# Attention over two layers on one core: single-head exponentials in three banks, four banks for the maxima jobs, and TensorE's order written out

## The chip, the cores and the metric

One core of a Trainium2 chip runs the whole kernel. The metric is the time of one execution on the device in microseconds (us), the median of several runs. TensorE (PE in the profile) multiplies matrices into PSUM, which has eight banks of 512 fp32 columns; VectorE (DVE) and ScalarE (ACT) read PSUM; GpSimd (POOL) works on SBUF; SP issues the transfers.

## The reference

The input x has 4 sequences of 1024 rows of 128 values. Four blocks follow, each added to x: attention a, a feed-forward block, attention b (causal), the same feed-forward block. Each works on the rows after a layer norm. Both attentions have 16 heads of 8 values.

```python
x = x + attn_a(layernorm(x))     # softmax(q k^T / sqrt(8)) v, then Wout
x = x + ffn(layernorm(x))        # (silu(x Wg^T) * (x Wu^T)) Wd^T, hidden 384
x = x + attn_b(layernorm(x))     # the same with keys after the query masked out
x = x + ffn(layernorm(x))
```

## The kernel before

An attention is worked off in 16 windows: a window is one sequence and four heads. Its two halves f are the query chunks of 512. For the softmax the kernel first finds each query's largest score, then computes the scores again, transposed, with that maximum taken off inside the product.

- A **job** (`run_job`, L995 on TensorE) is the scores of 128 queries of one head against up to 512 keys, into one PSUM bank. VectorE reduces it to a maximum per query (L785; where the causal mask cuts the block, L782). A window has 64 jobs in the first layer (`PLANS[0]`) and 48 in the second (`PLANS[1]`, widths 128 to 512). Jobs run in a ring of three banks, 4 to 6: the load of job k waits (`ring_free`) until VectorE has finished job k-3. In the first layer they go head by head, two key halves each.
- When the jobs of a half are through, VectorE negates the maxima (L791), GpSimd splits them (L463, L465), TensorE transposes them (the **shift**, L1027), ScalarE copies them (L575) and SP writes them as two more rows of the query operand `qop` (L373). The scores of that half wait for this transfer (`shift_loaded`).
- A **step** is one half against one block of 128 keys: 16 steps in the first layer, 12 in the second, where the triangular ones are narrower and get mask matmuls (L1017). In it the **scores** (L1009) are made for two heads at a time, a **unit**, into two banks; two units take turns, banks 0, 1 and 2, 3. ScalarE makes the exponentials of both heads in one instruction (L559).
- The weighted **sums** (L1045) multiply the step's exponentials by the values, in four column strips at once, into bank 7. They come one step behind. The values are copied for each window into `vwin` by GpSimd (L454).
- At the end of a half ScalarE copies the sums out (L566), TensorE transposes them (the **norm**, L938), ScalarE copies the result (L580), VectorE takes the reciprocal (L796) and multiplies (L801).

Heads with an even number use the lower 64 rows of the array, those with an odd number the upper 64; I call these the row halves 0 and 1. Jobs and scores use a row half each; sums, shifts and norms use all rows.

`Plan` decides what stands between what. It spreads the jobs over a step's four places in the proportions of `SLOT_WEIGHTS`, by width, so that in the first layer each step reads: job, two scores, two jobs, two scores, job, sums. In `turn` every engine walks through the plan in the same order. TensorE issues in that order, and each instruction waits for its own semaphores, so what stands behind a waiting one waits as well.

Of the kernel before, what the change touches and what calls it, by code (L numbers as in the profile page):

```python
# [13 lines left out]
P = 128  # L14
# [15 lines left out]
HG = 4  # L30
# [15 lines left out]
RING = 3  # L46
PROBS = 6
SLOT_WEIGHTS = (1, 1, 1, 0)
# [3 lines left out]
class Plan:  # L52
# [9 lines left out]


    def __init__(self, causal, turn, cut, idle_steps, lead, project_at):
        self.causal = causal
        self.turn = turn
# [12 lines left out]
        for f in range(2):  # L79
            for qb in range(TPC):  # L80
                for c in range(HG):
                    width = (TPC * f + qb + 1) * P if causal else S
                    for kh in range(2):
                        w = min(width - kh * CHUNK, CHUNK)
                        if w > 0:
                            stream.append((f, c, qb, kh, w, causal and kh * CHUNK + w == width))
        cut = len(stream) if cut is None else cut
        jobs = [(0, x) for x in stream[cut:]] + [(1, x) for x in stream[:cut]]
        self.turn_steps = [(0, s) for s in range(turn, n)] + [(1, s) for s in range(turn)]

        slots = [0 if i >= n - idle_steps else weight * (CHUNK - self.steps[s][2])
                 for i, (_, s) in enumerate(self.turn_steps) for weight in SLOT_WEIGHTS]
        total_c, total_s = sum(x[4] for _, x in jobs), sum(slots)
        placed, k, done_c, done_s = [], 0, 0, 0
        for w in slots:
            done_s += w
            slot = []
            while k < len(jobs) and (done_c + jobs[k][1][4] / 2) * total_s <= done_s * total_c:
                slot.append(jobs[k])
                done_c += jobs[k][1][4]  # L100
                k += 1
            placed.append(slot)
        assert k == len(jobs)
        self.turn_jobs = [placed[4 * i: 4 * i + 4] for i in range(n)]

        self.turn_ends = [[] for _ in range(n)]
        for i, (dw, s) in enumerate(self.turn_steps):

            if (dw, s) == (0, self.half_end[0] + 2):
                self.turn_ends[i].append((0, "norm", 0))  # L110
            if (dw, s) == (1, 1):
                self.turn_ends[i].append((0, "norm", 1))
            for jw, x in (y for slot in self.turn_jobs[i] for y in slot):
                if self.ends_half(x):
                    self.turn_ends[i + 1].append((jw, "shift", x[0]))


        units = [("exp", s, pair) for s in range(turn) for pair in range(2)]
        events, due, start = [], {}, None
        for k, x in enumerate(stream[:cut]):  # L120
            events.append(("job", x))
            if self.ends_half(x):
                due[k + 4] = ("shift", x[0])
                start = k + 4 + lead if x[0] == 0 else start
            if k in due:
                events.append(due.pop(k))
            elif start is not None and k >= start and (k - start) % 3 == 0 and units:
                events.append(units.pop(0))
        self.before = events + units + list(due.values())


        self.project_at = project_at
        own = [i for i, (dw, _) in enumerate(self.turn_steps) if dw == 0]
        self.last_jobs = [[[x for x in slot if x[0] == 0] for slot in self.turn_jobs[i]] for i in own]
        self.last_ends = [[x for x in self.turn_ends[i] if x[0] == 0] for i in own]
        self.units_before = sum(kind != "job" for kind, *_ in self.before)
        self.units_turn = 2 * n + sum(map(len, self.turn_ends))
        self.units_all = (self.units_before + (WINDOWS - 1) * self.units_turn + 2 * len(own)
                          + sum(map(len, self.last_ends)) + 1)
        self.jobs_before, self.jobs_turn = cut, len(jobs)  # L140
        self.jobs_all = WINDOWS * len(stream)
        assert self.units_turn % 2 == 0

    def ends_half(self, job):
        f, c, qb, kh, _, _ = job
        return (c, qb, kh) == (HG - 1, TPC - 1, 0 if self.causal and f == 0 else 1)


PLANS = [Plan(causal=False, turn=3, cut=32 + 22, idle_steps=0, lead=7, project_at=(6, 8, 11)), Plan(causal=True, turn=2, cut=None, idle_steps=1, lead=12, project_at=(2, 4, 8))]


def transformer_pair_kernel(nc, x_in, wqkv_a, bqkv_a, wout_a, bout_a, wqkv_b, bqkv_b, wout_b, bout_b,
# [10 lines left out]
    with ExitStack() as ctx:  # L163
# [121 lines left out]
        def windows(eng, body, turns):  # L285

            for w in range(turns):
                body(w, w % BUFS, w // BUFS)
# [913 lines left out]
```

## Time and profile before

| | |
|---|---|
| median of 3 runs | 1573.65 us (1570.76 to 1574.26) |
| profiled execution | 1573.21 us, of which the span from first to last instruction is 1571.4 us |
| first layer's attention | about 73 to 820 us |
| second layer's attention | about 944 to 1478 us |
| TensorE, VectorE, ScalarE busy | 92%, 79%, 62% of the span |
| mean granted TensorE clock | 0.965 of 2.4 GHz |

A timeline row gives start, duration, engine, line, operation, destination and source, and how many instructions it merges; in brackets the idle time before it and who ended it. PEld is the load of a matmul's stationary operand, which carries the wait. Ends of matmuls are modelled.

### The profile page before, as it was taken

The numbers are of one execution on the slowest core, as the hardware profiler recorded it, in microseconds if no ns is written. First come the engines' busy times: TensorE is split into PE (matmuls) and PEld (weight loads), VectorE is DVE, ScalarE is ACT, GpSimd is POOL, SyncE is SP. The second block draws the span as 40 slices with busy tenths as digits, with TensorE's granted clock in tenths as the row PEclk, the third lists the DMA queues.
The fourth block names the chain that finished last, engine by engine and source line by source line (L and its number), as shares of the span: only waits on it lengthen the run. The fifth ranks groups of instructions, "written<-read, shape, count | busy, mean of one in ns | idle before, by whom it ended". The sixth has DMA issues, their size and how long they took to land.

```text
span 1571.4 us, 26128 instructions
## 1 busy us (share of the span) xinstructions
PE 1438.6 (92%) x9625; PEld 701.7 (45%) x9625; DVE 1235.9 (79%) x3106; ACT 980.0 (62%) x1259; POOL 108.9 (7%) x210
## 2 busy tenths in 40 slices
PE   3699999999999999999988988999999999999888
PEld 2444344434444443444436654444444444444455
DVE  7589999999999998999937757787787877777254
ACT  4427777777777777777774432666666666666622
POOL 6020000000000000000001112000000000000010
PEclk9859999999999999999999985999999999999999
DMA  3720111111101111110001323111121112210000
GB/s 95 221 57 7 27 28 29 29 29 28 28 6 25 28 28 29 28 28 2 2 1 54 83 79 76 35 29 29 29 53 32 29 29 47 38 29 2 8 21 27
DMA packets 40055, 58.39 MB, mean 37 GB/s; under 512 B 7796, under 2 KB 19448, under 8 KB 39928
## 3 DMA queue, kind: packets, MB, share of 16 engines
q1 hardware_dynamic: 39928, 56.72, 15.2%
q8 instruction: 76, 1.25, 0.3%
q14 instruction: 51, 0.42, 0.1%
HBM read 36.77 MB, written 18.87 MB: 35 GB/s over the span
## 4 chain that ended last, share of the span: by engine, by line
PE 70%; DVE 18%; ACT 5%; issue 4%; DMA 2%; SPq 1%; POOL 0%; DVEq 0%; ACTq 0%; POOLq 0%
PE psum L995 25%; PE psum L1045 23%; DVE maxima L785 11%; PE psum L1009 6%; PE psum L1142 5%; PE psum L938 4%; ACT probs L559 3%; DVE junk L782 3%; PE psum L1147 2%; PE psum L1017 1%; PE psum L948 1%; DVE xn L706 1%; PE psum L1062 1%; DMA k_parts<-parts 1%; DMA qop<-shift_rows 1%
## 5 line engine op out<-in xcount | busy, mean ns | idle before, releaser
L559 ACT ACTIVATE probs<-psum 128x1024 f32<-128x1024 f32 (+3 forms) x896 | 794.2, 932 | 300.4 <-PE psum L1009 192.7
L785 DVE TENSOR_REDUCE maxima<-psum 128x1 f32<-128x512 f32 x1280 | 815.2, 684 | 72.8 <-PE psum L995 67.8
L995 PE MATMUL psum<-kop,qop 62*128 62x512 f32 (+3 forms) x1792 | 657.0, 465 | 56.5 <-DVE maxima L782 20.0
L1009 PE MATMUL psum<-qop,kop 64*128 64x512 f32 (+3 forms) x1792 | 498.2, 411 | 10.4 <-ACT probs L559 7.8
L995 PEld LDWEIGHTS psum<-kop,qop 62*128 62x128 f32 x1792 | 289.6, 191 | 487.6 <-DVE maxima L785 325.4
L1045 PE MATMUL psum<-probs,vwin 128*32 128x512 f32 (+3 forms) x3584 | 441.6, 565 | 3.9 <-ACT probs L559 2.0
L782 DVE CUSTOM_DVE_ANT_0 junk<-psum,mask 128x384 bf16<-128x384 f32 (+3 forms) x512 | 237.4, 487 | 75.3 <-PE psum L995 69.8
L1009 PEld LDWEIGHTS psum<-qop,kop 64*128 64x128 f32 x1792 | 242.0, 189 | 55.7 <-ACT probs L559 44.7
L1045 PEld LDWEIGHTS psum<-probs,vwin 128*32 128x32 f32 x3584 | 71.8, 109 | 105.5 <-issue 84.6
L1017 PE MATMUL psum<-half_ident,key_mask 64*128 64x64 bf16 x1024 | 92.7, 198 | 0.0
L1142 PE MATMUL psum<-ffn_xt,wffn 128*128 128x512 f32 x192 | 87.6, 594 | 0.0
L463 POOL TENSOR_TENSOR shift<-negmax,zeros 128x16 bf16<-128x16 f32 x64 | 14.1, 220 | 1017.5 <-DVE negmax L791 1017.5
L796 DVE RECIPROCAL rden<-att_raw 128x16 f32<-128x16 f32 x64 | 15.8, 247 | 61.3 <-ACT att_raw L580 61.3
L656 ACT ACTIVATE hid<-psum 128x512 f32<-128x512 f32 x48 | 28.7, 597 | 52.0 <-PE psum L1142 52.0
L1147 PE MATMUL psum<-wffn,hid 128*128 128x128 f32 x384 | 48.7, 278 | 7.9 <-DVE hid L899 7.9
L1017 PEld LDWEIGHTS psum<-half_ident,key_mask 64*128 64x128 bf16 x1024 | 49.7, 97 | 13.1 <-issue 1.3
L899 DVE TENSOR_TENSOR hid<-psum,hid 128x512 f32<-128x512 f32 x48 | 32.4, 689 | 26.8 <-PE psum L1142 21.4
L1147 PEld LDWEIGHTS psum<-wffn,hid 128*128 128x128 f32 x384 | 45.2, 192 | 15.4 <-DVE hid L899 15.4
L575 ACT CAST shift_rows<-psum 32x128 f32<-32x128 bf16 x64 | 16.3, 254 | 56.7 <-PE psum L1027 56.7
L714 DVE TENSOR_TENSOR x<-psum,x 128x512 f32<-128x512 f32 x32 | 22.1, 690 | 37.4 <-PE psum L1147 29.1
L1142 PEld LDWEIGHTS psum<-ffn_xt,wffn 128*128 128x128 f32 x192 | 34.2, 191 | 31.9 <-issue 31.0
L938 PEld LDWEIGHTS psum<-ident,sums 128*128 128x128 f32 x256 | 26.8, 140 | 44.9 <-ACT probs L559 40.2
(88 smaller groups left out, 709.9 us busy)
## 6 DMA issues: line engine op xcount, KB each, us to landing
qop<-q_parts SPq DMA_DIRECT2D x256, 64.0 KB
q_parts<-parts SPq DMA_DIRECT2D x32, 256.0 KB, 3.0
k_parts<-parts SPq DMA_DIRECT2D x32, 256.0 KB, 3.4
kop<-k_parts SPq DMA_DIRECT2D x64, 128.0 KB
kop<-k_parts SPq DMA_DIRECT2D x128, 64.0 KB
x<-in_L_attn_a_x SPq DMA_DIRECT2D x8, 256.0 KB, 4.4
qop<-shift_rows SPq DMA_DIRECT2D x128, 8.0 KB
out_x<-x SPq DMA_DIRECT2D x8, 256.0 KB, 2.3
```

Of the source, the lines that this page charges most:

```text
L559: nc.scalar.activation(probs[:, slot, :, c0:], psum[:, bank:bank + 2, c0:], ACT.Exp, scale=SCORE_SCALE).then_inc(probs_ready, 1)
L656: nc.scalar.activation(hid[:, c, :], psum[:, 2 + 2 * (c % 2), :], ACT.Silu).then_inc(silu_ready, 1)
L782: nc.vector.tensor_tensor_reduce(out=junk[:, slot, 0:width], in0=src, in1=mask[:, CHUNK - width:], scale=1.0, scalar=LOWEST, op0=ALU.add, ...
L785: nc.vector.tensor_reduce(dst, src, AX_X, ALU.max).then_inc(ring_free, 1)
L899: nc.vector.tensor_tensor(hid[:, c, :], psum[:, 3 + 2 * (c % 2), :], hid[:, c, :], ALU.mult).then_inc(hid_ready, 1)
L938: ins = nc.tensor.transpose(psum[:, bank, t * P:(t + 1) * P], src[:, t, :], ident[:])
L995: mm(psum[:, slot, 0:width], qop[rows, buf, f, r, qb * P:(qb + 1) * P].bitcast(F32R), kop[rows, buf, r, kh * CHUNK:kh * CHUNK + width].bit ...
L1009: ins = mm(psum[:, bank + h, c0:], kop[rows, buf, pair, j * P:(j + 1) * P].bitcast(F32R), qop[rows, buf, f, pair, c0:].bitcast(F32R), star ...
L1017: ins = mm(psum[:, bank + h, at:at + TILE_ROWS], key_mask[rows, part, :], half_ident[rows], start=False, stop=part == 1)
L1045: ins = mm(psum[32 * c:32 * c + 32, 7, c0:], vwin[:, buf, at:at + 32], probs[:, slot, c % 2, c0:], start=(j == 0), stop=(s == plan.half_en ...
L1142: mm(psum[:, 2 + 2 * (c % 2) + k, :], wffn[:, k, c, :], ffn_xt[:], start=True, stop=True).then_inc(gate_up_psum, 1)
L1147: ins = mm(psum[:, 7, t * P:(t + 1) * P], hid[:, c, t * P:(t + 1) * P], wffn[:, 2, c, :], start=(c == 0), stop=(c == FB - 1))
```

## The change

The plan is now a string of letters for each layer, walked by every engine: j is a job, s the scores of one unit, p the sums of the step that stands `sums_behind` steps back, H and h the shifts of this window's second and the next window's first half, N and n the norms.

In the first layer a unit is one head in one bank, `unit_ring=3`: banks 0 to 2; `job_ring=4`: banks 3 to 6. A step has four units and four exponentials of 512 columns. In the second layer units stay pairs in two double banks and jobs in three, but jobs are listed with `alternate=True`, so that neighbours use different row halves. The jobs run 48 ahead in the first layer and 44 in the second. The sums read `v` itself; `vwin` and its copies are gone. SP's loads of window w + 2 now come behind window w's second shift.

```diff
-RING = 3
-SLOT_WEIGHTS = (1, 1, 1, 0)
+PROB_STEPS = PROBS // 2
...
+                tiles = [(c, kh) for r in range(PAIRS) for kh in range(2) for c in (2 * r, 2 * r + 1)] if alternate \
+                    else [(c, kh) for c in range(HG) for kh in range(2)]
...
+    def bank(self, unit):
+        return unit % self.unit_ring * len(self.heads[0])
...
-PLANS = [Plan(causal=False, turn=3, cut=32 + 22, idle_steps=0, lead=7, project_at=(6, 8, 11)), Plan(causal=True, turn=2, cut=None, idle_steps=1, lead=12, project_at=(2, 4, 8))]
+PAIR_UNITS, HEAD_UNITS = ((0, 1), (2, 3)), ((0,), (1,), (2,), (3,))
+PLANS = [Plan(causal=False, heads=HEAD_UNITS, unit_ring=3, job_ring=4, alternate=False,
+              order="jsjjsspjssjsjpjsjsjnsjjsspjssjsjpjsjsjsjjsspjssjsjpHjsjsjsjjsspjssjsjpjsjsjsjjsspjssjsjpjsjsjNsjjsspjssjsjpjsjsjsjjsspjssjsjphjsjsjsjjsspjssjsjpjsjs",
+              jobs_ahead=48, sums_behind=2, project_at=(9, 11, 14)),
+         Plan(causal=True, heads=PAIR_UNITS, unit_ring=2, job_ring=3, alternate=True,
+              order="sjjsjpjsjsjpjjjHsjjsjpjsjjspjjsjsjsjjnjjspjsjsjjpjsjjsjpjjsjsjpjjsjNjjsphjjspjjjspjjspjs",
+              jobs_ahead=44, sums_behind=1, project_at=(4, 6, 10))]
...
                 for kind, w, number, f in plan.walk:
                     if kind == "shift":
-                        shift_to_operand(what[0], 0, unit)
...
+                        shift_to_operand(f, w % BUFS, unit_base + number)
+                        if f == 1 and w + 2 < WINDOWS:
+
+                            wait(sp, sums_done, sums_base + w * plan.n)
+                            load_operands(w + 2, (w + 2) % BUFS)
...
-                def exp_unit(w, wmod, s, pair, unit, static_unit):
+                def exp_unit(w, number, s, heads):
...
+                    if heads[0] == 0 and step >= PROB_STEPS:
+
+                        act.wait_ge(sums_done, sums_base + step + 1 - PROB_STEPS)
+                    nc.scalar.activation(probs[:, slot, heads[0] % 2:heads[-1] % 2 + 1, c0:], psum[:, bank:bank + len(heads), c0:],
+                                         ACT.Exp, scale=SCORE_SCALE).then_inc(probs_ready, 1)
...
-                        ins = mm(psum[32 * c:32 * c + 32, 7, c0:], vwin[:, buf, at:at + 32], probs[:, slot, c % 2, c0:],
+                        ins = mm(psum[32 * c:32 * c + 32, 7, c0:], v[:, at:at + 32], probs[:, slot, c % 2, c0:],
```

On TensorE, in the middle of the first layer, one step of before stands between two sums like this (L995 jobs, L1009 scores, L1045 sums):

```order
L1045 MATMUL psum<-probs,vwin 32x512 x4
L995 MATMUL psum<-kop,qop 128x512
L1009 MATMUL psum<-qop,kop 128x512 x2
L995 MATMUL psum<-kop,qop 128x512 x2
L1009 MATMUL psum<-qop,kop 128x512 x2
L995 MATMUL psum<-kop,qop 128x512
L1045 MATMUL psum<-probs,vwin 32x512 x4
```

There are four jobs and four scores between any two sums. In the changed kernel the same engine has, at the same place (L876 jobs, L890 scores, L924 sums), a group of ten, of which this is the whole:

```order
L924 MATMUL psum<-probs,v 32x512 x4
L876 MATMUL psum<-kop,qop 128x512
L890 MATMUL psum<-qop,kop 128x512
L876 MATMUL psum<-kop,qop 128x512
L890 MATMUL psum<-qop,kop 128x512
L876 MATMUL psum<-kop,qop 128x512
L890 MATMUL psum<-qop,kop 128x512
L876 MATMUL psum<-kop,qop 128x512 x2
L890 MATMUL psum<-qop,kop 128x512 x2
L924 MATMUL psum<-probs,v 32x512 x4
```

Behind its sums stands a group of six: job, two scores, job, score, job. The two kinds take turns, and a norm or shift goes into or ahead of one of ten.

In the second layer, on TensorE, before has in the middle of a window's second half (L938 is the norm):

```order
L1045 MATMUL psum<-probs,vwin 32x512 x4
L938 MATMUL psum<-ident,sums 128x128 x4
L995 MATMUL psum<-kop,qop 128x128
L995 MATMUL psum<-kop,qop 128x512
L1009 MATMUL psum<-qop,kop 128x512 x2
L995 MATMUL psum<-kop,qop 128x128
L995 MATMUL psum<-kop,qop 128x512
L1009 MATMUL psum<-qop,kop 128x512 x2
L995 MATMUL psum<-kop,qop 128x256
L995 MATMUL psum<-kop,qop 128x512
L1045 MATMUL psum<-probs,vwin 32x512 x4
```

It holds six jobs, and the group ahead of it and that behind it hold six as well. The changed kernel has there:

```order
L924 MATMUL psum<-probs,v 32x384 x4
L876 MATMUL psum<-kop,qop 128x128
L890 MATMUL psum<-qop,kop 128x512 x2
L876 MATMUL psum<-kop,qop 128x512
L890 MATMUL psum<-qop,kop 128x512 x2
L876 MATMUL psum<-kop,qop 128x512
L876 MATMUL psum<-kop,qop 128x128
L924 MATMUL psum<-probs,v 32x512 x4
L876 MATMUL psum<-kop,qop 128x128
L890 MATMUL psum<-qop,kop 128x512 x2
L876 MATMUL psum<-kop,qop 128x512 x2
```

The sums follow after four jobs instead of six. Ahead of this piece stands one long group of eight jobs, four pairs of scores and a norm.

## Rows read from the trace of the kernel before

**Rows 1.** The page, part 1: busy us, share of the span, instructions
```profile
PE 1438.6 (92%) x9625; PEld 701.7 (45%) x9625; DVE 1235.9 (79%) x3106; ACT 980.0 (62%) x1259; POOL 108.9 (7%) x210
```

**Rows 2.** The page, part 4: the chain that ended last, by line
```profile
PE psum L995 25%; PE psum L1045 23%; DVE maxima L785 11%; PE psum L1009 6%; PE psum L1142 5%; PE psum L938 4%; ACT probs L559 3%; DVE junk L782 3%; PE psum L1147 2%; PE psum L1017 1%; PE psum L948 1%; DVE xn L706 1%; PE psum L1062 1%; DMA k_parts<-parts 1%; DMA qop<-shift_rows 1%
```

**Rows 3.** Line L566, two stretches: duration min/median/max, first and last start
```profile
L566 ACT COPY sums<-psum x31: 585/587/596, 130.9 to 800.5; 128x512 f32<-128x512 f32 x31
L566 ACT COPY sums<-psum x21: 585/594/596, 1113.7 to 1431.3; 128x512 f32<-128x512 f32 x21
```

**Rows 4.** Waits from 200 to 700 us: total us, times, longest
```profile
PEld psum L995 <- DVE maxima L785: 213.5, 334, 0.8
```

**Rows 5.** Waits from 1010 to 1390 us
```profile
PEld psum L995 <- DVE maxima L782: 75.1, 155, 1.2
```

**Rows 6.** Timeline of one first-layer step, weight loads left out
```profile
410.17 0.51 PE L995 MATMUL psum<-kop,qop 62*128 62x512 f32 x1
410.17 0.74 PE L1009 MATMUL psum<-qop,kop 64*128 64x512 f32 x2
410.54 0.60 PE L995 MATMUL psum<-kop,qop 62*128 62x512 f32 x2
410.71 1.89 DVE L785 TENSOR_REDUCE maxima<-psum 128x1 f32<-128x512 f32 x3 [0.22 <-PE psum L995]
410.88 0.50 PE L1009 MATMUL psum<-qop,kop 64*128 64x512 f32 x2
410.94 1.94 ACT L559 ACTIVATE probs<-psum 128x1024 f32<-128x1024 f32 x2 [0.77 <-PE psum L1009]
411.46 0.50 PE L995 MATMUL psum<-kop,qop 62*128 62x512 f32 x1
411.88 1.07 PE L1045 MATMUL psum<-probs,vwin 128*32 128x512 f32 x8
412.88 0.50 PE L995 MATMUL psum<-kop,qop 62*128 62x512 f32 x1
```

**Rows 7.** Timeline: a norm between two steps
```profile
423.72 0.66 PE L938 MATMUL psum<-ident,sums 128*128 128x128 f32 x4
...
424.30 0.50 PE L995 MATMUL psum<-kop,qop 62*128 62x512 f32 x1
```

**Rows 8.** Exponentials of 512 elements: two in a row, and all (busy, mean ns)
```profile
1456.15 1.09 ACT L559 ACTIVATE probs<-psum 128x512 f32<-128x512 f32 x2
...
L559 ACT ACTIVATE probs<-psum 128x512 f32<-128x512 f32 x64 | 36.7, 597 | 31.0 <-PE psum L1017 30.9
```

**Rows 9.** Timeline: sums of steps without jobs, last window
```profile
791.93 1.06 PE L1045 MATMUL psum<-probs,vwin 128*32 128x512 f32 x8
...
793.98 1.06 PE L1045 MATMUL psum<-probs,vwin 128*32 128x512 f32 x8
```

**Rows 10.** A stretch: length, busy PE, PEld, DVE, ACT, POOL, granted clock, DMA share, GB/s
```profile
105.00:110.00 5.00, 5.00 (x19) 2.10 (x17) 4.47 (x8) 3.07 (x3) 2.39 (x1) 0.50 0.01 3
```

**Rows 11.** Groups by shape: masked maxima (busy us, mean ns, idle before)
```profile
L782 DVE CUSTOM_DVE_ANT_0 junk<-psum,mask 128x512 bf16<-128x512 f32 x128 | 85.6, 688 | 25.2 <-PE psum L995 22.5
L782 DVE CUSTOM_DVE_ANT_0 junk<-psum,mask 128x128 bf16<-128x128 f32 x128 | 34.2, 286 | 21.6 <-PE psum L995 19.4 <-issue 0.3
```

**Rows 12.** Timeline: sums of four successive steps of the second layer
```profile
1206.00 0.64 PE L1045 MATMUL psum<-probs,vwin 128*32 128x256 f32 x8
...
1208.25 0.85 PE L1045 MATMUL psum<-probs,vwin 128*32 128x384 f32 x8
...
1211.78 1.07 PE L1045 MATMUL psum<-probs,vwin 128*32 128x512 f32 x8
...
1215.47 1.07 PE L1045 MATMUL psum<-probs,vwin 128*32 128x512 f32 x8
```

**Rows 13.** Timeline: a shift, and the first scores that wait for it
```profile
415.47 0.22 PE L1027 MATMUL psum<-ident_bf,shift 128*32 128x128 bf16 x1
...
418.62 0.50 PE L1009 MATMUL psum<-qop,kop 64*128 64x512 f32 x2
```

More of the change, by code:

```diff
@@ L89, in __init__ @@
[L89 to L102, printed above, removed]
@@ L118, in __init__ @@
[L118 to L128, printed above, removed]
@@ L138, in __init__ @@
[L138 to L142, printed above, removed]
[L144 to L149 removed]
+                width = (TPC * f + qb + 1) * P if causal else S
@@ new lines, in __init__ @@
+        assert order.count("j") == len(stream) and order.count("s") == len(units) and order.count("p") == n
+        ends = {"H": ("shift", 0, 1), "h": ("shift", 1, 0), "N": ("norm", 0, 0), "n": ("norm", -1, 1)}
+        self.walk = []
+        jobs = taken = 0
+        last_unit = {}
+        for turn in range(-1, WINDOWS + 1):
+            j, u, k = jobs_ahead, 0, -sums_behind
+            for letter in order:
+                if letter == "j":
+                    w, x = turn + j // len(stream), stream[j % len(stream)]
+                    j += 1
+                    if 0 <= w < WINDOWS:
+                        self.walk.append(("job", w, jobs, x))
+                        jobs += 1
+                elif letter == "s":
+                    w, x = turn, units[u]
+                    u += 1
+                    if 0 <= w < WINDOWS:
+                        self.walk.append(("scores", w, taken, x))
+                        last_unit[w, x[0]] = taken
+                        taken += 1
+                elif letter == "p":
+                    w, x = turn + k // n, k % n
+                    k += 1
+                    if 0 <= w < WINDOWS:
+                        self.walk.append(("sums", w, last_unit[w, x], x))
+                else:
+                    kind, dw, f = ends[letter]
+                    if 0 <= turn + dw < WINDOWS:
+                        self.walk.append((kind, turn + dw, taken, f))
+                        taken += 1
@@ L881, in _ @@
-                invert_denominators(last, 1, unit)
-                scale_sums(last, 1)
+                unscaled, unnegated = [], []
+                for kind, w, number, what in plan.walk:
+                    if kind == "job":
+                        run_job(what, number)
+                    if kind in ("job", "sums", "shift"):
+                        for f, jobs in unnegated:
+                            negate_max(f, job_base + jobs)
+                        for window, f in unscaled:
+                            scale_sums(window, f)
+                        unscaled, unnegated = [], []
+                    if kind == "job" and plan.ends_half(what):
+                        unnegated.append((what[0], number + 1))
+                    if kind == "norm":
+                        invert_denominators(w, what, unit_base + number)
+                        unscaled.append((w, what))
+                    if kind == "scores" and w == WINDOWS - 1 and what[1] == plan.heads[-1]:
+                        early_chunk(what[0])
```

326 lines of the change are left out of this document (82 added, 244 removed).

## The prediction

> **What bounds the kernel now.** I read the page first. TensorE is busy 92% of the span and VectorE 79% [rows 1], but the chain that ended last is TensorE's jobs, TensorE's weighted sums, and VectorE's maxima in turn [rows 2]: a loop through two engines, not one full engine. The starts of the sums copies date the windows: 31 copies from 130.9 to 800.5 are 15 windows of 44.64 us in the first layer, 21 from 1113.7 to 1431.3 are 10 of 31.76 us in the second [rows 3]. In 500 us of the first layer TensorE's weight loads for jobs waited 213.5 us for VectorE [rows 4], in 380 us of the second 75.1 us for the masked maxima alone [rows 5].
>
> One step stands in [rows 6]. TensorE starts a job and the first scores at 410.17; the first job's maximum starts at 410.71, and the ring has three banks, so the step's fourth job waits for that maximum and loads at 411.46. It takes 0.42 to clear the array; the sums start at 411.88 and the next step 1.00 later, at 412.88. The loop is 0.54 + 0.75 + 0.42 + 1.00 = 2.71. VectorE's four maxima come 0.60 apart (three in 1.89, the last 0.69 long), 2.40 a step: it idles 0.22 before them. So 16 x 2.71 = 43.3, and two norms, each adding 0.58 (423.72 to 424.30, [rows 7]), make 44.5 of the 44.64.
>
> The same rows price TensorE. Matmuls of one row half end 0.24 apart: the first ends at 410.68, the scores at 410.91, the next job at 411.14, the last scores at 411.38, while matmuls of the other half run too. So halves run side by side, starts are in program order, and a 512-column matmul costs its half 0.24. A group between two sums costs 0.51 to its first end, 0.24 for each further one on the longer half, -0.07 to the sums (411.46 + 0.50 to 411.88), and 1.00.
>
> **The change, first layer.** The sums now have 3 and 5 jobs (and as many single scores) between them in turn. I write j and s with their row half. Long group: j1 s0 j1 s1 j0 s0 j0 j1 s1 s0; in-order starts put it in 6 places. Short group: j1 s1 s0 j0 s1 j0, 4 places.
> Long: without waits its last end is 0.51 + 5 x 0.24 = 1.71. Two rings bind. The fifth job needs the first's bank: as now, load at 0.54 + 0.75 = 1.29. The fifth scores need the second's bank out of three: first exponential at 0.54; the next 0.49 later (two in 1.09, one 0.60 long, [rows 8]), 1.03; it holds its bank 0.60, and a load follows its releaser by 0.05 to 0.06 (410.71 + 0.69 to 411.46); load at 1.69; sums 0.43 later, 2.12; group over at 3.12.
> Short: 0.51 + 3 x 0.24 - 0.07 = 1.16, plus 1.00 = 2.16; its banks have long been free.
> Two steps take 5.28, VectorE's eight maxima 4.80. A step is 2.64 against 2.71. The fourth bank removes the wait before every sums, but the score ring gives half of it back. A norm now stands inside a long group, after its third job: it starts at 0.51 + 2 x 0.24 - 0.07 = 0.92 and TensorE goes on 0.58 later, at 1.50; what is left, s0 j0 j1 s1 s0, takes 3 places, so the last end is 1.50 + 0.51 + 2 x 0.24 = 2.49 and the sums come at 2.42 instead of 2.12: 0.3 a norm, because the norm fills what was a wait. The rings don't bind there: the second bank's 1.69 is long past. Window: 8 x 5.28 + 2 x 0.3 = 42.85, or 1.8 less; 15 windows give 27 us. ScalarE: 64 exponentials x 0.49 = 31.4 and 3 for copies, under 42.9: hidden. The copies of v on GpSimd that go away were off the chain.
> Against the norm's new place speaks that it empties the array once more: 0.42 - 0.24 = 0.18 before it (a job alone clears the array in 0.42, in a stream costs 0.24) and 0.51 - 0.24 = 0.27 behind it [rows 6]. Without the wait that they fall into, a norm would cost 0.58 + 0.45 = 1.03, and the window would gain 1.8 - 1.4 = 0.4. This is what a rule of the Trainium skill says (TensorEngine Tiling (Array Packing), Key Properties): changing the tiling mode drains TensorE. I keep 0.3.
> Ends. In the last window most steps have no jobs. Now such steps take 2.05 (791.93 to 793.98, [rows 9]); after, long group 0.54 + 0.49 + 0.65 + 0.43 + 1.00 = 3.1 and short 0.51 + 0.24 - 0.07 + 1.00 = 1.7, 2.4 a step: 12 x 0.35 = +4. The prefix runs jobs alone at VectorE's 0.60 and gives 6 jobs less but 3 steps less too; the clock there is at 1.2 GHz (0.50 from 105 to 110, [rows 10]), and the first full steps fall in it: +2, an estimate. First layer: -27 + 6, rounded -20 us.
>
> **The change, second layer.** Three banks and pairs stay; what changes is the order, and jobs now alternate halves. The loop above, with VectorE's times for masked jobs (688 ns for 512 columns, 286 for 128, so 0.134 per 128 columns, each 0.08 less start to start [rows 11]: 0.61, 0.48, 0.34, 0.21), says a group of n jobs takes 0.54 + the first n-3 maxima + 0.15 + 0.42 + the sums (1.00, 0.79, 0.57, 0.36 by width: four passes of 53 ns less for every 128 columns). They are checked by [rows 12], from one sums to the next (the sums in the formula are those that the interval begins with). To 1208.25, four jobs: 0.48 + 1.11 + 0.57 = 2.16, measured 2.25. To 1211.78, six: 0.61 + 0.60 + 0.21 + 1.11 + 0.79 = 3.32, measured 3.53. To 1215.47, six and a norm: 0.21 + 0.60 + 0.21 + 1.11 + 1.00 + 0.58 = 3.71, measured 3.69. So this layer is one ring wait per group, and the more jobs stand between two sums, the longer it is: VectorE idles through the sums, then TensorE waits through its maxima.
> The maxima of a window sum to 16 x 0.60 + 8 x (0.61 + 0.48 + 0.34 + 0.21) = 22.7, with its small operations about 24.2. The new order puts eight jobs, four score pairs and a norm into one long group and two to five jobs into each other one. I walked it with the same rules, carrying VectorE's backlog over each sums.
> The long group: its first job ends at 0.47, and the maxima run on from 0.50 at 0.48, then 0.61 and 0.60 each. Exponentials of a pair start 0.92 apart (two in 1.94, the last 1.02, [rows 6]) and hold their bank 1.02 + 0.05: they start at 0.79 and 1.71, so the third pair loads at 1.86 and the norm at 2.78. It is over at 3.36; the two jobs and the last scores behind it end at 4.10, the sums (384 wide) come at 4.03 and end at 4.8. VectorE has never been idle and has work until 5.2.
> Then, in order: 2.15, 2.05, 2.6, 3.3 (with the other norm), 1.8, 1.65, 1.2, 2.3, 2.3, 1.95, 1.75. With 4.8 that is 27.9. E.g. the group after the long one, j1.128 s s j0.512 s s j1.512 j0.128: the backlog is 0.4, every bank is free before it is needed, last end 0.36 + 0.16 + 3 x 0.24, 1.15 to the sums, + 1.00 = 2.15 where the old order has 3.5 to 3.7. My rules ran short of [rows 12] by 0.09, 0.21 and -0.02, 0.1 on average; on 12 groups that makes 29.1. Gain 2.6 a window, 15 windows: 39. Ends: two more steps in the last window, +3.5; prefix 44 jobs instead of 48 with two steps at half clock, -4.5. Second layer: -40 us.
> Moved too: a half's shift goes through TensorE, ScalarE and SP's queue before its first scores; now that takes 3.15 us from its transpose to the scores that wait for it (415.47 to 418.62, [rows 13]). In the new order 4.0 lie between in the second layer and over 5 in the first, so it hides; were it late, the excess would be paid twice a window. SP's 14 loads of a window now stand behind its second shift instead of ahead of it, a whole window before they are used: nothing.
>
> **Sum.** The profiled execution took 1573.2 (span 1571.4), the median is 1573.65: no difference. 1573 - 20 - 40 = 1513; I say 1515.
>
> **The rivals.**
> 1. The score ring is kinder or the waits merge: VectorE becomes the bound, 2.40 a step and 27 a window in the second layer. First layer 8 x 4.80 + 1.4 = 39.8 (-4.8 a window, 72 less, 6 lost at the ends), second 27 a window (-70): 1437 with both, 1480 for half of the way. For it: four banks cover a sums of 1.00. Against: the load at 1.69 that the score ring forces. Chance 0.1.
> 2. The first layer gains nothing: exponentials 0.60 apart instead of 0.49 lengthen each long group by 0.11 (14 us), and a third of the drain is paid after all (6 us). With the second layer whole it is 1535, with half of its gain 1553. For it: a single exponential's records are 0.60 long, and no first-layer row shows two behind each other. Chance 0.17.
> 3. Slower: single scores lose their side-by-side partner. Today scores come as a pair, one on each half; if a job beside a score does not overlap, or a same-half load is exposed, places become more. Price: a further place is 0.24 in two steps, and there are 128 such pairs of steps: 31 us. From two further places on it decides (1515 + 62 = 1577); with three the time is 1607, and fully serial, 16 places for 10, 1515 + 184 = 1700. Against it, [rows 6] have a job and a score loading at 410.17 together, and the same-half ends 0.24 apart. Chance 0.08.
> It is also what a rule of the Trainium skill would do here (TensorE: Matmul & The Clock Gate, Part 3, The mechanism): a weight load overlaps matmuls in flight only where the row group differs. The trace disagrees with it: its same-half ends stand 0.24 apart, 512 columns at 2.4 GHz being 0.213, with a load between each two.
> 4. The time does not move, the waits only change places: 0.03.
>
> **How the numbers follow.** Likeliest (0.62): both layers gain, 1495 to 1540. A measurement here tells 0.2% (3 us). The range takes in half of rival 1 and most of rival 2: 1485 to 1555. Faster: 0.62 + 0.1 + 0.16 = 0.88; same 0.03; slower 0.09.
>
> **What would show it.** First layer: sums copies 42.9 apart per window; sums alternately 3.1 and 2.15 apart; TensorE's longest wait in the long group for the exponential, not for the maximum. Second: windows near 29, VectorE's share of them up. Wrong: more than 0.24 between same-half ends, exponentials 0.6 apart, or jobs waiting again ahead of each sums.

## The result, and the profile of the changed kernel

The changed kernel takes 1464.33 us (median of 4 runs, 1462.78 to 1466.14); before, run beside it, takes 1573.95 (4 runs, 1570.76 to 1577.89). The ratio is 0.9303, 95% interval 0.9279 to 0.9327: 110 us less, where I had said 1515 and a range from 1485. The forecast had the sign and half of the size.

The page of the changed kernel, part 1, and the chain that ended last, by engine and by line:

```profile
PE 1374.2 (94%) x9625; PEld 683.6 (47%) x9625; DVE 1226.2 (84%) x3106; ACT 1001.4 (68%) x1771; POOL 94.4 (6%) x178
...
PE 82%; DVE 8%; ACT 5%; issue 2%; DMA 1%; SPq 1%; POOL 1%; DVEq 0%; ACTq 0%; POOLq 0%
PE psum L924 26%; PE psum L876 24%; PE psum L890 15%; PE psum L989 5%; DVE maxima L703 4%; PE psum L819 4%; ACT probs L498 4%; PE psum L994 3%; PE psum L829 2%; PE psum L898 2%; DVE xn L624 1%; PE psum L941 1%; DVE junk L700 1%; DMA k_parts<-parts 1%; ACT ot L528 1%
```

VectorE's maxima, 11% of the chain of before [rows 2], are 4% of this one; TensorE's scores went from 6% to 15%. The chain has moved into TensorE. The busy times of VectorE and ScalarE hardly changed [rows 1]: the same work in less idle time.

The sums copies (L505, L566 before) date the windows again. Changed kernel, two stretches, duration min/median/max, first and last start:

```profile
L505 ACT COPY sums<-psum x31: 600/604/607, 129.2 to 746.6; 128x512 f32<-128x512 f32 x31
```
```profile
L505 ACT COPY sums<-psum x21: 580/592/592, 1062.6 to 1341.1; 128x512 f32<-128x512 f32 x21
```

A first-layer window is (746.6 - 129.2) / 15 = 41.16 us against 44.64, a second-layer one (1341.1 - 1062.6) / 10 = 27.85 against 31.76 [rows 3]. Fifteen windows of each give 52 and 59 us; the ends of the layers give about 2 back. Waits of the changed kernel, total us, times, longest; the first three rows from 200 to 700 us, the last three from 960 to 1340:

```profile
PEld psum L876 <- DVE maxima L703: 181.4, 267, 0.8
...
PEld psum L890 <- ACT probs L498: 8.2, 49, 0.2
DVE maxima L703 <- PE psum L876: 4.3, 24, 0.2
```
```profile
PEld psum L876 <- DVE maxima L703: 50.9, 63, 0.8
PEld psum L876 <- DVE maxima L700: 49.4, 122, 0.8
DVE junk L700 <- PE psum L876: 35.6, 94, 0.7
```

The 181.4 us beside the 213.5 of [rows 4] look like little gained, but most of either is no wait for VectorE. The weight loads of the long group that is timed below:

```profile
401.95 0.18 PEld L876 LDWEIGHTS psum<-kop,qop 62*128 62x128 f32 x1 [0.84 <-DVE maxima L703]
...
403.23 0.18 PEld L876 LDWEIGHTS psum<-kop,qop 62*128 62x128 f32 x1 [0.48 <-DVE maxima L703]
```

The first is the load of a group's first job. Such a load comes 1.00 behind the start of the sums in every group that begins with a job, in both kernels, whether the maximum that frees its bank ended 0.07 before it, as here, or 0.43, as for the load at 400.05. Its pause is that of the sums. Of the 181.4 us 152.3 are of this kind; the other 29.1 are 73 fifth jobs, in the long groups without a norm, that load 0.04 after their maximum. Of the 213.5 before, 122.8 are of the first kind and 90.7 are the fourth job of each step. The wait for VectorE inside the groups fell from 90.7 to 29.1 us, and only long groups have it.

VectorE's listed waits are 4.3 us in 500: it runs nearly through, busy 40.5 of a window's 41.2 us, where it was 40.7 of 44.7. One short and one long group, timeline of the changed kernel, weight loads left out, columns as in [rows 6]:

```profile
400.05 0.50 PE L876 MATMUL psum<-kop,qop 62*128 62x512 f32 x1
400.06 0.73 PE L890 MATMUL psum<-qop,kop 64*128 64x512 f32 x2
400.39 0.40 PE L876 MATMUL psum<-kop,qop 62*128 62x512 f32 x1
400.59 3.79 DVE L703 TENSOR_REDUCE maxima<-psum 128x1 f32<-128x512 f32 x6 [0.18 <-PE psum L876]
400.63 0.39 PE L890 MATMUL psum<-qop,kop 64*128 64x512 f32 x1
400.64 0.39 PE L876 MATMUL psum<-kop,qop 62*128 62x512 f32 x1
400.83 4.26 ACT L498 ACTIVATE probs<-psum 128x512 f32<-128x512 f32 x8 [0.60 <-PE psum L890]
400.96 1.07 PE L924 MATMUL psum<-probs,v 128*32 128x512 f32 x8
401.96 0.49 PE L876 MATMUL psum<-kop,qop 62*128 62x512 f32 x1
...
403.57 0.59 PE L890 MATMUL psum<-qop,kop 64*128 64x512 f32 x2
404.09 1.07 PE L924 MATMUL psum<-probs,v 128*32 128x512 f32 x8
...
405.08 0.50 PE L876 MATMUL psum<-kop,qop 62*128 62x512 f32 x1
```

The short group starts at 400.05; its six matmuls end at 400.55, twice 400.79, 401.02, 401.03 (start plus duration; two of the six are merged), three on each half, 0.24 apart. Its sums start 0.91 after it, the next group 1.91 after it. The long group goes from 401.96 to 405.08: 3.12, as worked out. ScalarE's eight exponentials take 4.26 us: starts 0.49 apart and 0.60 for the last would be 4.03, the rest is the wait for the long group's first scores. VectorE's maxima, 0.60 apart, fill 4.8 of the 5.04 of these two steps. A long group that holds a norm takes 3.56 from sums to sums, the others 3.14.

### The profile page after: what moved, and what is told of

It reads as the page before. It is cut to its first block, busy times and chain, and to the rows that moved or that the text cites. A ratio compares the mean times of both kernels' runs of the same rounds, so it can differ in the third digit from the quotient of the medians.

```text
span 1462.5 us, 26609 instructions
## 1 busy us (share of the span) xinstructions
PE 1374.2 (94%) x9625; PEld 683.6 (47%) x9625; DVE 1226.2 (84%) x3106; ACT 1001.4 (68%) x1771; POOL 94.4 (6%) x178
## 4 chain that ended last, share of the span: by engine, by line
PE 82%; DVE 8%; ACT 5%; issue 2%; DMA 1%; SPq 1%; POOL 1%; DVEq 0%; ACTq 0%; POOLq 0%
PE psum L924 26%; PE psum L876 24%; PE psum L890 15%; PE psum L989 5%; DVE maxima L703 4%; PE psum L819 4%; ACT probs L498 4%; PE psum L994 3%; PE psum L829 2%; PE psum L898 2%; DVE xn L624 1%; PE psum L941 1%; DVE junk L700 1%; DMA k_parts<-parts 1%; ACT ot L528 1%
## 5 line engine op out<-in xcount | busy, mean ns | idle before, releaser
L498 ACT ACTIVATE probs<-psum 128x512 f32<-128x512 f32 (+3 forms) x1408 | 833.6, 658 | 216.4 <-PE psum L890 116.3
L703 DVE TENSOR_REDUCE maxima<-psum 128x1 f32<-128x512 f32 x1280 | 805.1, 682 | 20.5 <-PE psum L876 15.0
L876 PE MATMUL psum<-kop,qop 62*128 62x512 f32 (+3 forms) x1792 | 592.4, 449 | 18.0 <-DVE v L643 11.1
L890 PE MATMUL psum<-qop,kop 64*128 64x512 f32 (+3 forms) x1792 | 527.1, 422 | 6.4 <-ACT probs L498 2.5
L876 PEld LDWEIGHTS psum<-kop,qop 62*128 62x128 f32 x1792 | 283.7, 192 | 402.7 <-DVE maxima L703 299.0
L924 PE MATMUL psum<-probs,v 128*32 128x512 f32 (+3 forms) x3584 | 440.4, 564 | 0.6 <-ACT probs L498 0.5
L890 PEld LDWEIGHTS psum<-qop,kop 64*128 64x128 f32 x1792 | 268.7, 187 | 76.1 <-ACT probs L498 45.3
L700 DVE CUSTOM_DVE_ANT_0 junk<-psum,mask 128x384 bf16<-128x384 f32 (+3 forms) x512 | 233.5, 485 | 50.3 <-PE psum L876 46.5
L924 PEld LDWEIGHTS psum<-probs,v 128*32 128x32 f32 x3584 | 70.9, 108 | 101.0 <-issue 67.5
L632 DVE TENSOR_TENSOR x<-psum,x 128x512 f32<-128x512 f32 x32 | 22.1, 690 | 36.8 <-PE psum L994 29.1
L819 PE MATMUL psum<-ident,sums 128*128 128x128 f32 x256 | 41.1, 283 | 5.0 <-ACT sums L505 1.6
```

The source lines that it names most:

```text
L498: nc.scalar.activation(probs[:, slot, heads[0] % 2:heads[-1] % 2 + 1, c0:], psum[:, bank:bank + len(heads), c0:], ACT.Exp, scale=SCORE_SCA ...
L700: nc.vector.tensor_tensor_reduce(out=junk[:, slot, 0:width], in0=src, in1=mask[:, CHUNK - width:], scale=1.0, scalar=LOWEST, op0=ALU.add, ...
L703: nc.vector.tensor_reduce(dst, src, AX_X, ALU.max).then_inc(ring_free, 1)
L819: ins = nc.tensor.transpose(psum[:, bank, t * P:(t + 1) * P], src[:, t, :], ident[:])
L876: mm(psum[:, bank, 0:width], qop[rows, buf, f, r, qb * P:(qb + 1) * P].bitcast(F32R), kop[rows, buf, r, kh * CHUNK:kh * CHUNK + width].bit ...
L890: ins = mm(psum[:, bank + k, c0:], kop[rows, buf, c // 2, j * P:(j + 1) * P].bitcast(F32R), qop[rows, buf, f, c // 2, c0:].bitcast(F32R), ...
```

## The experiments

Times with three rounds have an interval; single ones (E3 to E7) are compared with before's 1570 to 1581. "Two steps" is always one long and one short group, and window lengths are distances of sums copies.

**E1 and E2: one layer at a time.** The other layer gets the order of before, rebuilt as a string of letters, with the reciprocal as late as it was. Here for E1:

```diff
-         Plan(causal=True, ..., alternate=True, order="sjjsjpjsjsjpjjjHsjjsjp...", jobs_ahead=44, ...)]
+         Plan(causal=True, ..., alternate=False, order="sjjsjpsspHnjjjsjjsjpjj...", jobs_ahead=45, ..., late=(6, 0))]
```

> The first layer as in the changed kernel, the second layer with the order of before (jobs not alternating, the reciprocal as late as it was). Theory A (each layer's gain stands by itself, 3.5 us a window in the first): windows of 41.2 us in the first layer and 31.7 in the second, in all 1573 - 54 = 1520 us. Rival (the layers help each other, or the second layer gains from what is common, the missing copies of v and the later loads): second-layer windows clearly under 31.7, below 1505 us.

> The second layer as in the changed kernel; the first layer with the order of before, pairs in two double banks and three job banks. Theory A: windows of 44.6 us in the first layer and 27.9 in the second, in all 1573 - 55 = 1518 us; together with the other half run this makes the whole 109 us. Rival: less than 40 us gained, the rest being common to both.

E1: 1510.3 (1509.65 to 1510.67), ratio 0.9594 (0.9577 to 0.9611). E2: 1517.5 (1516.81 to 1518.62), 0.9640 (0.9619 to 0.9661). So 64 and 56 us, together 10 more than both at once. In E1's trace the first-layer windows are 41.18 as in the changed kernel, but the second layer with its old order has windows of 31.40 instead of 31.74 (5 us in 15), and 162.0 instead of 165.1 us lie between the last sums copy of one layer and the first of the next, where the changed kernel has 166.2. So some 8 us of E1's gain are not the first layer's order, and E1 lands between the theory's 1520 and the rival's 1505. The 5 us stand in windows in which TensorE has the same order as before; the edits outside the order (no `vwin` copies, other times for SP's loads) are left for them, but none was tried by itself. The 3 us needn't be theirs: the rebuilt layer starts another way, with 45 jobs ahead of its first scores where before had 32. In E2 the rebuilt first layer has windows of 44.82 instead of 44.66, 2.5 us in 15. Why the new second-layer order doesn't have the 8 us on top was not separated either.

**E6 and E7: the second layer's order without alternating halves, and the reverse.**

E6 is E1 with the first change here, E7 the changed kernel with the second:

```diff
-              alternate=False, order="sjjsjpsspHnjjjsjjsjp...",
+              alternate=True, order="sjjsjpsspHnjjjsjjsjp...",
...
-              alternate=True, order="sjjsjpjsjsjpjjjHsjjsjp...",
+              alternate=False, order="sjjsjpjsjsjpjjjHsjjsjp...",
```

> The first layer as in the changed kernel; the second with the order of before, but jobs alternate between the row halves. Theory A (the order makes the gain, since jobs waited for banks and not for a half): second-layer windows 31.3 to 31.7 us, 1510 to 1520 in all. Rival (the alternation makes a good part of it): windows under 30 us, under 1495.

> The changed kernel, but in the second layer jobs go head by head. Theory A (the order makes the gain): second-layer windows 27.9 to 28.5 us, 1464 to 1474 in all. Rival (the alternation makes a good part): 29.5 us or more, 1490 or more.

E6: 1531.1, 21 us more than E1, windows 32.2 to 34.9; both its theory (1510 to 1520) and its rival missed. E7: 1471.8, 7 us more than the changed kernel, windows 28.65. The second layer's gain is the order; alternation is worth 7 us with it, and costs 21 with the old one.

E6's 21 us are two things. At full clock its windows are 32.2 against 31.4, 12 us in 15. The excess stands in two of the twelve groups, 3.93 and 3.90 where E1 has 3.54 and 3.46. In the first of them the alternating list puts a job of 512 columns third, where E1 has one of 128, and the sixth job waits for the third's maximum: 0.61 - 0.21 = 0.40 by the prices of [rows 11], an estimate, 0.39 measured. So there it is the width of a job, not its half, that costs; the second group was not worked out. The other 9 us fall into windows in which TensorE's clock drops to 0.50. Three stretches as in [rows 10], E6, E6, and the changed kernel:

```profile
1030.00:1150.00 120.00, 110.53 (x991) 56.86 (x990) 92.40 (x310) 76.16 (x112) 3.51 (x16) 1.00 0.14 30
1161.00:1163.00 2.00, 2.00 (x11) 0.61 (x4) 0.32 (x1) 0.00 (x0) 0.00 (x0) 0.50 0.04 8
```
```profile
1000.00:1340.00 340.00, 336.98 (x3255) 178.51 (x3247) 300.65 (x1045) 246.59 (x365) 10.62 (x48) 1.00 0.18 37
```

E6's second layer has seven such stretches, one of 6.8 us at 963 and six of 3.4 us at 997, 1024, 1161, 1195, 1324 and 1359. E1's has one, at 1081, and before has one of 6.8 us at 1108, where two overlapping spans of a window take 33.9 and 34.2 instead of 31.7.

**E3: the halves made uneven.** Only the first layer's list of jobs changes:

```diff
-Plan(causal=False, heads=HEAD_UNITS, unit_ring=3, job_ring=4, alternate=False,
+Plan(causal=False, heads=HEAD_UNITS, unit_ring=3, job_ring=4, alternate=True,
```

> The changed kernel with one number different: the first layer's jobs are listed in alternating row halves too; order, rings and second layer stay. Theory A (the row halves are two independent queues; a group without waits costs 0.20 + 0.2365 x the matmuls on the fuller half + 1.00): the short group's five matmuls behind its first are then 4 on one half and 2 on the other instead of 3 and 3, so it takes 2.14 instead of 1.90 us from sums to sums; in the long group the first scores stand behind a job of their own half, their exponential starts 0.24 later and so does the load that waits for the second exponential, 3.38 instead of 3.14. Two steps 5.5, a first-layer window about 45, the kernel about 1520. Rival B (single scores run beside anything, only a wait can cost): the short group stays at 1.90; only the later exponential counts, at most 1.9 a window, about 1493. Rival C (the half of a job is of no account in this layer): 1464.

1510.75, windows 44.11. E3's timeline, one short group and the start of the next:

```profile
399.78 0.50 PE L876 MATMUL psum<-kop,qop 62*128 62x512 f32 x1
399.79 0.73 PE L890 MATMUL psum<-qop,kop 64*128 64x512 f32 x2
400.13 0.40 PE L876 MATMUL psum<-kop,qop 62*128 62x512 f32 x1
400.36 0.39 PE L890 MATMUL psum<-qop,kop 64*128 64x512 f32 x1
...
400.58 0.39 PE L876 MATMUL psum<-kop,qop 62*128 62x512 f32 x1
400.90 1.07 PE L924 MATMUL psum<-probs,v 128*32 128x512 f32 x8
401.90 0.51 PE L876 MATMUL psum<-kop,qop 62*128 62x512 f32 x2
```

The same six matmuls with four on one half: 2.12 from group to group instead of 1.91, one place more (400.97 is the last end). The long groups take 3.33 to 3.37 instead of 3.14 to 3.17. Theory A had 2.14 and 3.38. Nothing but the list of jobs was changed, and it costs 46 us. With starts in program order the short group takes four places with either list, so nothing would change in it: this is the run that shows that the halves are independent queues and that the fuller one sets the length. The window is 44.1 and not 45 because the groups are 0.06 a pair shorter than worked out (0.5) and a norm costs 0.17 here where I had left it 0.4 (0.5).

**E4: four banks for scores, three for jobs.**

```diff
-heads=HEAD_UNITS, unit_ring=3, job_ring=4, alternate=False,
+heads=HEAD_UNITS, unit_ring=4, job_ring=3, alternate=False,
```

> The changed kernel with the first layer's seven banks divided the other way: four for single scores, three for jobs; order unchanged. Theory A (the score ring and the job ring bind the long group at almost the same point): the fourth job of the long group now waits for the first maximum and the fifth for the second: load at 1.89 instead of 1.29, sums at 2.3 to 2.55, two steps 5.4 to 5.5, a window of 43.9 to 45, the kernel 1505 to 1520. Rival (the score ring alone makes the long group long, VectorE has slack): two steps below 5.04, the kernel below 1464.

1498.7, windows 43.60, both a little under the range that I gave. Short groups 1.90, long ones 3.54 to 3.57 (A: 3.57). Waits of E4, 200 to 650 us:

```profile
PEld psum L876 <- DVE maxima L703: 182.6, 289, 0.8
...
PEld psum L890 <- ACT probs L498: 3.4, 20, 0.2
```

The same row of the changed kernel has 163.5 us in this stretch. Without the first jobs of the groups it is 51.8 in E4, at the fourth and fifth jobs, against 25.9: here the job ring alone sets the long group. All eight long groups are equally long, those with a norm too: there the norm costs nothing.

**E5: even groups.**

```diff
-order="jsjjsspjssjsjpjsjsjnsjjsspjssjsjp..."
+order="sjsjsjjspsjsjsjjspsjsjnsjjsp..."
```

> The changed kernel with the first layer's jobs and scores spread evenly, four jobs and four single scores between any two sums (scores, job, scores, job, scores, job, job, scores), rings as in the changed kernel. Theory A: the fourth scores need the bank of the first of the same group, whose exponential starts at about 0.54 and holds it 0.6, so they load at 1.19 and the sums start at 1.62: each step takes 2.6, two steps 5.2 instead of 5.04, a window 42.6, the kernel about 1485. Rival (the fourth bank for the jobs is the whole gain, and the split into 3 and 5 is of no account): 5.04 for two steps, 1464.

1500.4, windows 43.32; I had said 1485 and 42.6. E5's timeline, sums, a group without a norm, one with (L819), sums:

```profile
409.30 1.07 PE L924 MATMUL psum<-probs,v 128*32 128x512 f32 x8
...
411.90 1.07 PE L924 MATMUL psum<-probs,v 128*32 128x512 f32 x8
...
413.79 0.66 PE L819 MATMUL psum<-ident,sums 128*128 128x128 f32 x4
...
415.27 1.07 PE L924 MATMUL psum<-probs,v 128*32 128x512 f32 x8
```

A step takes 2.60, as A said (2.62 from the fourth scores' wait). With the norm it takes 3.37, 0.77 more, which I had not counted: two norms a window make 1.5 of the 1.7 by which the window exceeds 16 x 2.60. Splitting four and four into five and three lets one group in two go without any wait. Even groups, with the fourth bank and single scores, keep 1.3 us of the window's gain of 3.5; the split makes the other 2.2.

**E8: the second layer with single heads as well.**

```diff
-Plan(causal=True, heads=PAIR_UNITS, unit_ring=2, job_ring=3, alternate=True, order="sjjsjp...",
+Plan(causal=True, heads=HEAD_UNITS, unit_ring=3, job_ring=4, alternate=True, order="ssjjssjp...",
```

> The changed kernel with the second layer's seven banks divided as in the first: single heads in three banks, jobs in four; every scores letter is written twice, else the same order. What still waits in that layer is the load of jobs for maxima (85 us of 320). Theory A (the wait for the job ring bounds this layer): the fourth bank takes away part of it, the score ring of three gives some back: windows 26.5 to 28.5 instead of 27.83, the kernel 1445 to 1475. Rival (exponentials of one head cost ScalarE more, masks overlap less, and the score ring binds in every group): windows over 29, the kernel over 1480.

1515.3 (1510.73 to 1516.14), ratio 0.9608 (0.9574 to 0.9643), windows 31.19: the rival. Waits of E8, 1010 to 1390 us:

```profile
PEld psum L890 <- ACT probs L498: 55.6, 136, 0.9
PEld psum L876 <- DVE maxima L700: 53.3, 87, 0.8
```

The jobs' waits did not go, and the longest of TensorE's is now that of scores for a bank, 55.6 us; the same row of the changed kernel, from 960 to 1340 us, has 11.1. The letters were doubled without a new arrangement, so this says nothing of the best order for single heads.

**E9: the theory used for an order.** If a group of three and three costs 1.90 and only the n-th scores beyond the third wait, then one group of seven and three of three (4.12 + 3 x 1.90 = 9.82 by the rule) are cheaper than two of five and two of three (10.08).

```diff
-Plan(causal=False, heads=HEAD_UNITS, unit_ring=3, job_ring=4, alternate=False,
+Plan(causal=False, heads=HEAD_UNITS, unit_ring=3, job_ring=4, alternate=True,
+              order="jsjspjsjsjspjsjsjsnjsjsjsjspjsjsjspjsjsjspjsjsjspHjsjsjsjsjsjsjspjsjsjspjsjsjspjsjsjspjsjsjsNjsjsjsjspjsjsjspjsjsjspjsjsjsphjsjsjsjsjsjsjspjsjsjspjs",
+              jobs_ahead=49, sums_behind=2, project_at=(9, 11, 14)),
```

> The changed kernel with a new order for the first layer: one group of seven jobs and seven single scores, then three groups of three and three, jobs and scores taking turns letter by letter; jobs alternate halves, so that each short group has three on either half; 49 jobs ahead; the norms and shifts in or ahead of the groups of seven; second layer untouched. Theory A (independent halves; the n-th scores of a group wait for the exponential n-3 places earlier, one each 0.49 us; only a group with more than three pays): short groups 1.90; in the long group the seventh scores load at 0.54 + 3 x 0.49 + 0.65 = 2.68, sums at 3.12, over at 4.12. Four steps take 4.12 + 3 x 1.90 = 9.82 instead of 10.08, a window 39.3 and about 0.8 for norms and shifts, 40.1 instead of 41.18: 1450 for the kernel. VectorE's 64 maxima (38.4) and small operations (1.4) forbid less than 39.8. Rival (what counts is how evenly VectorE is fed; a group of seven starves it afterwards): the short groups wait for maxima, windows at 41 or more, 1462 to 1480.

1448.6 (1446.97 to 1449.88), ratio 0.9215 (0.9198 to 0.9231): 1% below the changed kernel, whose interval it does not touch. Copies of E9, first layer, and its timeline from the last scores of a long group through a short one:

```profile
L505 ACT COPY sums<-psum x31: 587/598/599, 129.1 to 730.6; 128x512 f32<-128x512 f32 x31
```
```profile
402.05 0.50 PE L890 MATMUL psum<-qop,kop 64*128 64x512 f32 x1
...
402.54 0.50 PE L890 MATMUL psum<-qop,kop 64*128 64x512 f32 x1
402.96 1.06 PE L924 MATMUL psum<-probs,v 128*32 128x512 f32 x8
...
403.96 0.50 PE L876 MATMUL psum<-kop,qop 62*128 62x512 f32 x1
...
405.86 0.50 PE L876 MATMUL psum<-kop,qop 62*128 62x512 f32 x1
```

Windows (730.6 - 129.1) / 15 = 40.10, forecast 40.1. The last scores load 2.70 after the group's start (399.84 to 402.54; 2.68 by the rule), one exponential (0.49) behind those at 402.05; the long group takes 4.12, the short one 1.90. VectorE's line in the same stretch is one row of 19 maxima in 11.76 us without a pause. It is busy 39.98 of a window's 40.10 us, so it has no slack left. Nor has TensorE's order, whose rule gives 40.1 by itself; which of the two would have to give way first isn't shown.

**E10: E9, and a second layer found by the same rules.** Letters were moved at random and each order priced by the rules, until a window cost 1.06 less than the changed kernel's.

```diff
-              order="sjjsjpjsjsjpjjjHsjjsjpjsjjspjjsjsjsjjnjjspjsjsjjpjsjjsjpjjsjsjpjjsjNjjsphjjspjjjspjjspjs",
-              jobs_ahead=44, ...
+              order="sjjsjjspjjsjsjjHjjnjjspjsjsjpjsjjspjsjpjjsjsjjphjjjssjpsjjjpjjssjjpjjNjsjsjpjjssjpjjspjs",
+              jobs_ahead=45, ...
```

> As the run before it, and the second layer in an order of its own that was found by moving letters and pricing each order by the same rules (independent halves, rings, VectorE's and ScalarE's times as measured); jobs 45 ahead. Its groups have two to nine jobs, the norms stand in two different long groups. Theory A: by these rules a second-layer window takes 1.06 less than the changed kernel's 27.83, so 26.8; with the first layer as in the run before, the kernel is at about 1435. Rival (the rules are good for explaining an order but not for finding one, small terms pile up): 27.5 to 29 a window, 1445 to 1465.

1449.1 (1447.75 to 1451.94), ratio 0.9223 (0.9202 to 0.9245): no gain over E9. Ordinary windows are 27.6 to 27.75 instead of 26.8, and beside the first three of 15 are 29.2 to 29.35. The group that holds a shift, a norm and nine jobs takes 3.9 where the rules gave 3.4; most others are within 0.2. A stretch with one of the long windows, length, busy times, granted clock, DMA share and GB/s last, as in [rows 10]:

```profile
1060.00:1074.00 14.00, 13.80 (x152) 7.97 (x148) 12.91 (x44) 9.54 (x17) 0.44 (x2) 1.00 0.01 3
1074.00:1075.00 1.00, 1.00 (x8) 0.70 (x7) 1.00 (x6) 0.05 (x1) 0.00 (x0) 0.97 0.00 0
1075.00:1078.00 3.00, 3.00 (x18) 1.05 (x19) 1.53 (x8) 0.88 (x2) 0.00 (x0) 0.50 0.32 88
```

TensorE's clock falls to 0.50 (1.2 GHz) for 3.4 us at 1075, and again at 1188 and 1300; these are the three long windows, 1.5 us each. Two more such stretches, at 935 and 1328, stand near the layer's ends. The changed kernel's second layer has none between 940 and 1360 us, and one at 1369. The rest of the shortfall, 27.7 for 26.8, is at full clock and belongs to the rules.

## Why the prediction was wrong

**What bounds the kernel** was read rightly: a ring wait between TensorE and VectorE at every sums, not a full engine.

**The step that failed** is the reading of [rows 6] as "halves run side by side, starts are in program order", and the count of places that followed: 4 for the short group. Counted in places, each the 0.24 that a matmul takes of its half, both readings give four for those rows. But [rows 6] merge two jobs into their third row, and the trace of before has them apart:

```profile
410.54 0.50 PE L995 MATMUL psum<-kop,qop 62*128 62x512 f32 x1
410.75 0.40 PE L995 MATMUL psum<-kop,qop 62*128 62x512 f32 x1
```

In the order j1 s0 s1 j1 j0 s0 s1 the job of half 1 comes first, and it stands behind the scores of its half, which end at 410.91: it is the one that ends 0.24 later, at 411.14. The job of half 0 comes after it in the program and starts 0.20 before it. So the rows of before, taken one by one, already spoke against starts in program order, and I missed it. In the changed kernel the short group j1 s1 s0 j0 s1 j0 has three matmuls on either half and takes three places: 1.90, not 2.16. The halves keep their own queues, and neither waits for the other's starts. E3 settles it: with four on one half the same letters take 2.12. The rule that E3, E4 and E9 bear out is: a group without waits takes 0.20 + 0.24 x (matmuls on the fuller half) + 1.00.

In the sum this term is (2.16 - 1.90) x 8 = 2.1 a window, 31 us. Against it stand a long group of 3.14 for 3.12 (0.2 a window) and a norm of 0.42 for 0.3 (0.2 a window); that makes the 1.7 between 42.85 and 41.16, 25 us in 15 windows.

**The long group** was right in mechanism and size: 3.12 worked out, 3.14 measured, the fifth scores waiting for the second exponential, and the exponentials 0.49 apart (rival 2 had 0.60). The mark that I gave for it was not: I wrote that the longest wait there would be for the exponential, but inside the groups the profile books 29.1 us to the maxima and 8.2 to the exponentials, because the fifth job's wait, to a load at 1.27, stands ahead of the fifth scores' and leaves only the rest up to 1.70 to these. The prediction also took all 213.5 us of [rows 4] for waits for VectorE; 90.7 were. Its sum doesn't use that number. E4 and E9 show both rings at work.

**The norm** was to cost 0.3, or 1.03 if the array's emptying is paid in full. It costs 0.00 in E4, 0.17 in E3, 0.42 in the changed kernel, 0.77 in E5, by how much of a wait it falls into. No run here shows one without any wait, so the full price stays unmeasured; what the sum needed was the size of the wait. That changing the tiling mode drains TensorE is the Trainium skill's rule (TensorEngine Tiling (Array Packing), Key Properties); these runs neither refute it nor price it.

**The ends of the first layer** were to lose 6 us and gained 1.5: the first window's copy comes 1.7 earlier (129.2 for 130.9, [rows 3]), and the last half loses 0.1. I had taken 2.05 for each of its steps from [rows 9]; the eight between the last two copies took 18.83, 2.35 each, and take 18.95 now.

**The second layer's walk** gave 27.9 a window, and 27.85 is measured. The step that failed here is the allowance of 0.1 a group that I put on top from [rows 12], 1.2 a window, 18 us. Those rows are groups of the old order, and their shortfall did not carry over. The agreement of the sum is partly luck: single groups were off by up to 0.8 both ways (2.3 and 1.95 worked out for two neighbours, 1.61 and 2.77 measured), and E10, where I trusted the rules for an order of my own, was 0.8 a window short.

**Sum.** First layer -54 for -20: 25 the windows, 7.5 the ends, the rest rounding. All else -55 for -40: 19 the allowance, less 4 at the ends.

**The rivals.** Rival 1 had the time, 1437 to 1480, and I gave it 0.1. In the first layer its engine is close to the bound, busy 40.5 of 41.2 us a window. In the second it is not: VectorE is busy 24.65 of 27.84, TensorE 27.61, and no row gives the 27 that the rival named. What I held against it, the load at 1.69, is real and costs only the long group. Rivals 2 and 4 are out. Rival 3, and with it the Trainium skill's rule that a load overlaps only matmuls of another row group (TensorE: Matmul & The Clock Gate, Part 3, The mechanism), is refuted by the same-half ends 0.24 apart in the short group above, with a load of 0.18 to 0.19 between each two: that of the second matmul on half 1 runs from 400.16 to 400.35, while the first streams until 400.55. The range failed at its lower end because the count of places, the allowance and the ends all erred on the dear side.

## What to carry to other kernels

When two row halves of TensorE are in use, count the matmuls of each half between two full-array stops, and balance the halves there: one place too many costs its full time, and where no bank is waited for the first layer's short groups show nothing else of the order that matters (1.90 for three different orders of three and three). Where a bank is waited for, the widths count too: one wide job that moved forward cost E6 0.39 us in its group. When a ring is shorter than a step needs, gather the surplus in one group and let the others stay under the ring's length, with transposes and other full-array work in the long one; E9 is the case, and its window was forecast within 0.1 us by that rule. And an allowance made from groups of the old order belongs into the range, not into the forecast.

## What the runs showed of the hardware

- Matmuls on different row halves do not wait for each other's starts: six matmuls of 512 columns clear the array 0.91 us after the first start with three on each half, 1.12 with four on one.
- A program's later matmul can start before an earlier one, if it is on the other row half: by 0.20 us in before, at 410.54.
- Between a weighted sums and the load of the next job lie 1.00 us in both kernels. The profile books that pause to VectorE's maximum even where it ended 0.43 before.
- TensorE's clock drops to 1.2 GHz for 3.4 or 6.8 us in the middle of work in several of these second layers: seven times in E6, five in E10, once in before and in E1, once at the end of the changed kernel. A denser order doesn't explain it: between drops TensorE is busy 92% in E6 (110.5 of 120 us), 99% in E10 (106.0 of 107), and 99% in the changed kernel (337.0 of 340), which has none there. A drop of 3.4 us costs E10 1.5. What makes the difference is open.
